# Split attention probabilities: transposed by TensorE, or laid out by one transposing DMA a head

## The chip, the cores and the metric

One core of a Trainium2 chip runs the kernel. The metric is the device time of one execution in microseconds (us); smaller is better. Engines are called as the profile calls them: PE is TensorE (PEld its weight loads), ACT ScalarE, DVE VectorE, POOL GpSimd, SP SyncE, whose queue (SPq) issues all DMAs here.

## The reference

Thirty-two batches of 256 tokens with 512 features, and 16 heads of 32 features each:

```python
h = jnp.maximum(_layernorm(x, axis=-1), 0.0)
q = split_heads(h @ Wq.T); k = split_heads(h @ Wk.T); v = split_heads(h @ Wv.T)
bias = (adj + adj)[:, None]
a = jnp.einsum('bhnd,bhmd->bhnm', q, k) * scale + bias
row_nonzero = jnp.any(a != 0, axis=-1, keepdims=True)
a = jnp.where(row_nonzero, a, -jnp.inf)
p = jax.nn.softmax(a, axis=-1)
p = jnp.where(jnp.isnan(p), 0.0, p)
o = jnp.einsum('bhnm,bhmd->bhnd', p, v)
x = x + (o @ Wo.T)
```

## The kernel before, in words

Precision comes from splitting: each operand of a product is kept as a high part and a low part, and three products are added (high by high, high by low, low by high). A split takes two passes: ACT copies the value rounded (`..._hi`), DVE subtracts that from the value (`..._lo`).

The work of a batch is laid out in 16 **slots**, one a head, and each engine has its own hand-written queue of slots (`body` in the block of each engine). In slot hh:

- PE transposes the probabilities of head hh into PSUM (`transpose_probs`, L401, four 128x128 blocks), computes the scores of head hh + 3 (`scores`, L390), in even slots the values of heads hh - 2 and hh - 1 (`values`, L422 and L423, 16 small f16 matmuls for two heads), and then the piece of the projections that the table `JOBS` gives this slot (`job`, L328). A job is a tuple (kind, number, batch offset, first product, end): `qk` is a projection to queries and keys of four heads (24 products of 256 columns), `v` a part of the values (12 products), `y` half of the output projection (12 products of 512 columns), `h` and `o` transposes of the normalised tokens and of the attention output.
- DVE adds the adjacency to the scores of head hh + 2 and finds the row bound (`shift`, L703), does its half of the splits of the jobs that ended in the slot before (`take`), and then the low half of the probabilities of head hh (`low_probs`, L721).
- ACT copies finished values out of PSUM in odd slots (`copy_outputs`, L542), takes the exponentials of head hh + 1 (`exponentials`, L553, two instructions, one for each 128 rows), does its half of the takes (L519, L520 for `qk`), and then the high half of the probabilities of head hh (`high_probs`, L564).
- POOL folds the shifted scores for the test of empty rows (`fold`), divides by the row sums (`divide`), normalises the next tokens and adds the residual.
- SP loads and stores, and rearranges finished queries and keys into `qk_stack` (`stack`, L252): twice a batch, 12 DMAs in one piece, each to 32 partitions.

The exponentials write an SBUF tile `probs` of two buffers. PE transposes from it into the PSUM tile `pT_ps` of two banks, and both halves of the split are made there and land in `pT_hi` and `pT_lo` (f16, four buffers each), the stationary operands of `values`. What orders the heads is this: the exponentials of head n + 1 wait for the transposes of head n - 1,

```python
act.wait_ge(pT_ready, head_no(b, hh) - 1)
```

and those of head n for the split of head n - 2. PSUM has eight banks: three for scores, two for `pT_ps`, one for the values, two for jobs.

## Time and profile before

| | |
|---|---|
| median of 3 runs | 1320.17 us (1317.58 to 1320.48) |
| the profiled execution's own time | 1319.87 us |
| its span | 1318.1 us |
| busy in the span | PE 1288.6 us (98%), DVE 1130.4 (86%), ACT 1033.8 (78%), POOL 902.1 (68%) |
| DMA engines | 47.9% of 16 engines' span, for 163.64 MB |
| granted clock of PE | 0.996 of full speed, mean over the run |

The profile gives one execution. Busy times are unions of the instructions' spans: two instructions of one engine can overlap by some 0.1 us, so the distance from one start to the next is what an instruction costs its engine, and its own span is when its result is there. The 32 batches make a steady loop; a short stretch in front splits the weights and fills the pipeline, and one behind drains it.

### The profile page before, as it was taken

How to read it: one execution, taken by the hardware profiler on the slowest of the kernel's cores; microseconds unless marked ns; L12 is line 12 of the kernel's file. 1: busy time of each engine (PE TensorE's matmuls, PEld its weight loads, DVE VectorE, ACT ScalarE, POOL GpSimd, SP SyncE). 2: the span in 40 equal slices, each digit the busy share in tenths (PEclk: the TensorE clock that was granted, in tenths of full speed). 3: DMA queues.
4: the chain of work that ended last, by engine and by line, in shares of the span. 5: the costliest groups of instructions: out<-in, count | busy, mean ns of one | idle time of the engine just before them, and what ended most of it. 6: DMA issues, size and time to landing. Idle time of an engine off the chain costs nothing. (4 is left out here: it accounts for less than half of the span.)

```text
span 1318.1 us, 43774 instructions
## 1 busy us (share of the span) xinstructions
PE 1288.6 (98%) x13072; PEld 1225.6 (93%) x13072; DVE 1130.4 (86%) x4023; ACT 1033.8 (78%) x2379; POOL 902.1 (68%) x1263
## 2 busy tenths in 40 slices
PE   5899999999999999999999999999999999999996
PEld 5899999999999999999999999999999999999995
DVE  5888888888888888888889888888888888888884
ACT  3788778788787888887888787888788887788874
POOL 5667667667677676676776676776677776676765
PEclk9999999999999999999999999999999999999998
DMA  6445454455354454454454454454544554544441
GB/s 213 104 117 138 108 136 119 115 139 127 109 146 117 109 148 119 112 143 116 114 151 109 122 130 121 123 143 108 131 119 122 133 133 110 139 119 113 126 121 49
DMA packets 90772, 163.88 MB, mean 124 GB/s; under 512 B 14976, under 2 KB 23168, under 8 KB 90752
## 3 DMA queue, kind: packets, MB, share of 16 engines
q1 hardware_dynamic: 90752, 163.64, 47.9%
q8 instruction: 10, 0.16, 0.1%
q14 instruction: 10, 0.08, 0.0%
HBM read 46.14 MB, written 16.78 MB: 48 GB/s over the span
## 5 line engine op out<-in xcount | busy, mean ns | idle before, releaser
L849 POOL TENSOR_TENSOR fold<-minus 128x512 f32<-128x512 f32 x256 | 329.7, 1288 | 325.3 <-DVE bounds L703 325.3
L553 ACT ACTIVATE probs<-minus,bounds 128x256 f32<-128x256 f32 x1024 | 460.2, 500 | 19.1 <-DVE bounds L703 19.1
L564 ACT ACTIVATE pT_hi<-pT_ps 128x512 f16<-128x512 f32 x512 | 306.0, 598 | 154.3 <-PE pT_ps L401 152.6
L721 DVE TENSOR_TENSOR pT_lo<-pT_ps,pT_hi 128x512 f16<-128x512 f32 x512 | 351.1, 686 | 84.5 <-ACT pT_hi L564 84.2
L703 DVE CUSTOM_DVE_ANT_0 minus<-s_ps,adj_now 128x256 f32<-128x256 f32 x1024 | 389.3, 417 | 18.3 <-DVE adj_now L715 14.3
L401 PE MATMUL pT_ps<-ident,probs 128*128 128x128 f32 x2048 | 307.6, 273 | 1.7 <-ACT probs L553 1.6
L328 PE MATMUL job_ps<-hT_hi,w_hi 128*128 128x256 f32 x1024 | 300.4, 293 | 3.1 <-DVE hT_lo L671 2.6
L328 PE MATMUL job_ps<-hT_lo,w_hi 128*128 128x256 f32 x1024 | 290.1, 283 | 0.0
L328 PE MATMUL job_ps<-hT_hi,w_lo 128*128 128x256 f32 x1024 | 289.8, 283 | 0.0
L401 PEld LDWEIGHTS pT_ps<-ident,probs 128*128 128x128 f32 x2048 | 240.4, 140 | 15.4 <-ACT probs L553 2.6
L390 PE MATMUL s_ps<-qk_stack 96*128 96x256 f32 x1024 | 247.1, 323 | 2.2 <-DMA qk_stack<-qk_parts 2.2
L855 POOL TENSOR_TENSOR bounds<-fold 128x256 f32<-128x256 f32 x256 | 189.3, 740 | 24.9 <-POOL fold L849 9.5
L328 PEld LDWEIGHTS job_ps<-hT_hi,w_hi 128*128 128x128 f32 x1024 | 194.8, 190 | 3.8 <-issue 3.8
L328 PEld LDWEIGHTS job_ps<-hT_hi,w_lo 128*128 128x128 f32 x1024 | 196.0, 191 | 0.0
L328 PEld LDWEIGHTS job_ps<-hT_lo,w_hi 128*128 128x128 f32 x1024 | 195.8, 191 | 0.0
L390 PEld LDWEIGHTS s_ps<-qk_stack 96*128 96x128 f32 x1024 | 154.8, 191 | 2.7 <-DMA qk_stack<-qk_parts 2.6
L422 PE MATMUL o_ps<-v_parts,pT_hi 128*128 128x65 f16 x2048 | 153.6, 192 | 1.4 <-DVE pT_lo L721 1.0
L423 PE MATMUL o_ps<-v_parts,pT_lo 128*128 128x33 f16 x2048 | 147.5, 179 | 0.0
L328 PE MATMUL job_ps<-w_hi,hT_lo 128*128 128x256 f32 x512 | 147.4, 288 | 0.0
L328 PE MATMUL job_ps<-w_hi,hT_hi 128*128 128x256 f32 x512 | 147.3, 288 | 0.1
L328 PE MATMUL job_ps<-w_lo,hT_hi 128*128 128x256 f32 x512 | 144.3, 282 | 0.0
L422 PEld LDWEIGHTS o_ps<-v_parts,pT_hi 128*128 128x128 f16 x2048 | 123.6, 96 | 14.3 <-DVE pT_lo L721 1.5
(80 smaller groups left out, 2406.4 us busy)
## 6 DMA issues: line engine op xcount, KB each, us to landing
qk_stack<-qk_parts SPq DMA_DIRECT2D x768, 128.0 KB, 2.3
x_in<-x SPq DMA_DIRECT2D x32, 512.0 KB, 3.4
x_res<-x SPq DMA_DIRECT2D x32, 512.0 KB, 3.6
out<-y SPq DMA_DIRECT2D x64, 256.0 KB, 2.1
adj_in<-adj SPq DMA_DIRECT2D x32, 256.0 KB, 3.6
minus<-wq_t SPq DMA_DIRECT2D x2, 512.0 KB, 6.0
qk_parts<-wv SPq DMA_DIRECT2D x2, 512.0 KB, 10.5
y<-wk_t SPq DMA_DIRECT2D x1, 512.0 KB, 8.4
```

The source lines that it names most:

```text
L328: end = nc.tensor.matmul(dst, lhs[a](k), rhs[c](k), start=i == 0, stop=i == len(terms) - 1)
L390: end = nc.tensor.matmul(s_ps[SCORE_BANK[hh]][:, t * N:(t + 1) * N], stack[:, 0, t * P:(t + 1) * P], stack[:, 1, :], start=True, stop=True)
L401: end = nc.tensor.transpose(pT_ps[hh % 2][:, m * N + t * P:m * N + (t + 1) * P], probs[hh % 2][:, t, m * P:(m + 1) * P], ident[:, :])
L422: nc.tensor.matmul(ps[:, 0:LOW + HD], hi, v[:, 0:LOW + HD], start=m == 0, stop=False)
L423: end = nc.tensor.matmul(ps[:, 0:HD + 1], lo, v[:, 0:HD + 1], start=False, stop=m == NT - 1)
L553: end = nc.scalar.activation(probs[hh % 2][:, t, :], minus[hh // 2 % 2][:, hh % 2, t, :], ACT.Exp, bias=bounds[:, hh // 2 % 4, 2 * (hh % 2 ...
L564: nc.scalar.activation(pT_hi[hh % 4][:, :, :], pT_ps[hh % 2][:, :].rearrange("p (m n) -> p m n", m=NT), ACT.Copy).then_inc(pT_high, 1)
L703: end = nc.vector.tensor_tensor_reduce(out=minus[pair % 2][:, hh % 2, t, :], in0=s_ps[SCORE_BANK[hh]][:, t * N:(t + 1) * N], in1=adj_now[: ...
L721: nc.vector.tensor_tensor(pT_lo[hh % 4][:, :, :], pT_ps[hh % 2][:, :].rearrange("p (m n) -> p m n", m=NT), pT_hi[hh % 4][:, :, :], ALU.sub ...
L849: nc.gpsimd.tensor_tensor(f1[:, :, :], src[:, :, 0:N // 2], src[:, :, N // 2:N], ALU.add).then_inc(folded1, 1)
L855: nc.gpsimd.tensor_tensor(f2, f1[:, :, 0:N // 4], f1[:, :, N // 4:N // 2], ALU.add).then_inc(folded2, 1)
```

## The change

- The exponentials write to PSUM (`probs`, two banks, in the natural layout: rows on partitions). ACT copies the high half from there and DVE subtracts the low half into one SBUF tile `p_parts` (f16, both halves, four buffers).
- SP then issues one transposing DMA a head (`turn_probs`): it reads `p_parts` (128 partitions, 1024 f16 each, 256 KB) and writes `pT` as eight blocks of 128x128, what `values` takes as stationary operands. PE's `transpose_probs` is gone. `values` runs two slots later (heads hh - 4 and hh - 3), and with it `copy_outputs`, `any_nonzero`, `factors` and `divide`.
- Scores have two banks in place of three, jobs three in place of two.
- The products of `qk` and `v` take f16 operands: `hT`, and the weights scaled to powers of two. For it, all three of Wq, Wk, Wv are scaled by rows and transposed by PE in the stretch in front, as only Wv was before.
- The table of jobs is new. `qk` jobs now end in slots 1, 7, 9 and 11, `v` jobs in 2, 3 and 15 (two), `o` in 6 and 14, `y` in 12 and 13. The copy of the adjacency moves from DVE to ACT, in slot 13; the statistics of the tokens on DVE move from slot 0 to slot 6.
- SP's queue carries the 16 transposing DMAs of a batch in slot order; the two bursts of stack DMAs stand behind those of heads 1 and 9.

```diff
-PRODUCTS = {"qk": 24, "v": 12, "y": 12, "h": 1, "o": 1}
+W_TOP, H_TOP = 2.0 ** 14, 2.0 ** 9
+PRODUCTS = {"qk": 24, "v": 12, "y": 12, "h": 4, "o": 4}
 JOBS = {
-    0: [("qk", 3, 0, 0, 12)],
-    1: [("qk", 3, 0, 12, 24), ("v", 2, 0, 0, 2)],
+    0: [("qk", 3, 0, 0, 13)],
+    1: [("qk", 3, 0, 13, 24), ("v", 2, 0, 0, 2)],
     2: [("v", 2, 0, 2, 12), ("v", 3, 0, 0, 3)],
...
+    6: [("qk", 0, 1, 6, 16), ("o", 1, -1, 0, 4)],
+    7: [("qk", 0, 1, 16, 24), ("qk", 1, 1, 0, 6)],
+    8: [("qk", 1, 1, 6, 18)],
...
+            def turn_probs(b, hh, early):
+                sp.wait_ge(p_split, head_no(b, hh) + 1)
+                settled(sp, "sp")
+                if not early:
+                    sp.wait_ge(pv_done, head_no(b, hh) - 3)
+                    settled(sp, "sp")
+                sp.dma_start_transpose(pT[hh % 4][:, :, :],
+                                       p_parts[hh % 4][:, :, :, :].rearrange("p a t n -> p (a t n)")
+                                       ).then_inc(p_turned[hh % 4], 16)
             def body(b, first, last):
-                if not last:
-                    sp.wait_ge(adj_copied, b + 1)
-                    settled(sp, "sp")
-                    sp.dma_start(adj_in[:, :, :], adj_d[b + 1]).then_inc(adj_loaded, 16)
-                stack(1, b, first)
-                if not (last or isinstance(b, int) and b + 2 == B):
-                    load_tokens(b + 2)
-                if not first:
-                    store(b - 1, 0)
-                if not last:
-                    stack(0, b + 1, False)
-                if not first:
-                    store(b - 1, 1)
-                    sp.dma_start(x_res[:, :, :], x_d[b]).then_inc(res_loaded, 16)
+                for hh in range(HEADS):
+                    turn_probs(b, hh, first and hh < 4)
+                    if hh == 0 and not last:
+                        sp.wait_ge(adj_copied, b + 1)
+                        settled(sp, "sp")
+                        sp.dma_start(adj_in[:, :, :], adj_d[b + 1]).then_inc(adj_loaded, 16)
+                        if not (isinstance(b, int) and b + 2 == B):
+                            load_tokens(b + 2)
+                    if hh == 1:
+                        stack(1, b, first)
+                    if hh == 9 and not last:
+                        stack(0, b + 1, False)
+                    if hh == 14 and not first:
+                        store(b - 1, 0)
+                    if hh == 15 and not first:
+                        store(b - 1, 1)
+                        sp.dma_start(x_res[:, :, :], x_d[b]).then_inc(res_loaded, 16)
...
-            def transpose_probs(b, hh, early):
-                pe.wait_ge(exp_done, head_no(b, hh) + 1)
-                if not early:
-                    pe.wait_ge(pT_split, head_no(b, hh) - 1)
-                for m in range(NT):
-                    for t in range(NT):
-                        end = nc.tensor.transpose(pT_ps[hh % 2][:, m * N + t * P:m * N + (t + 1) * P],
-                                                  probs[hh % 2][:, t, m * P:(m + 1) * P], ident[:, :])
-                end.then_inc(pT_ready, 1)
...
-                pe.wait_ge(pT_split, head_no(b, hh) + 1)
+                pe.wait_ge(p_turned[hh % 4], b * HEADS * 4 + (hh // 4 + 1) * 16)
                 for t in range(NT):
                     q = (hh % 2) * NT + t
                     ps = o_ps[:, q * P:(q + 1) * P]
                     for m in range(NT):
-                        hi = pT_hi[hh % 4][:, m, t * P:(t + 1) * P]
-                        lo = pT_lo[hh % 4][:, m, t * P:(t + 1) * P]
+                        hi, lo = (pT[hh % 4][:, (part * NT + t) * NT + m, :] for part in range(2))
...
-                    for was in range(hh - 2, hh) if hh % 2 == 0 else ():
...
+            def scale_weight(i, half):
+                act.wait_ge(w_scales, TURNS.index((i, half)) + 1)
+                for k in range(2 * half, 2 * half + 2):
+                    end = nc.scalar.activation(w_in[i][:, k, :], w_in[i][:, k, :], ACT.Copy,
+                                               scale=w_scale[:, i, UNSCALE, k:k + 1])
+                end.then_inc(w_scaled, 1)
...
                 if not early:
-                    act.wait_ge(pT_ready, head_no(b, hh) - 1)
+                    act.wait_ge(p_split, head_no(b, hh) - 1)
                 for t in range(NT):
-                    end = nc.scalar.activation(probs[hh % 2][:, t, :], minus[hh // 2 % 2][:, hh % 2, t, :], ACT.Exp,
+                    end = nc.scalar.activation(probs[hh % 2][:, t * N:(t + 1) * N], minus[hh // 2 % 2][:, hh % 2, t, :], ACT.Exp,
                                                bias=bounds[:, hh // 2 % 4, 2 * (hh % 2) + t, BOUND:BOUND + 1],
                                                scale=-1.0)
                 end.then_inc(exp_done, 1)
             def high_probs(b, hh, early):
-                act.wait_ge(pT_ready, head_no(b, hh) + 1)
+                act.wait_ge(exp_done, head_no(b, hh) + 1)
                 if not early:
-                    act.wait_ge(pv_done, head_no(b, hh) - 3)
-                nc.scalar.activation(pT_hi[hh % 4][:, :, :], pT_ps[hh % 2][:, :].rearrange("p (m n) -> p m n", m=NT),
-                                     ACT.Copy).then_inc(pT_high, 1)
-            for half in range(2):
-                high_weight(WQ, half)
-            high_weight(WK, 0)
+                    act.wait_ge(p_turned[hh % 4], b * HEADS * 4 + hh // 4 * 16)
+                nc.scalar.activation(p_parts[hh % 4][:, 0, :, :], probs[hh % 2][:, :].rearrange("p (t n) -> p t n", t=NT),
+                                     ACT.Copy).then_inc(p_high, 1)
...
+                act.wait_ge(adj_loaded, (b + 1) * 16)
+                if not (isinstance(b, int) and b == 0):
+                    act.wait_ge(shifted, head_no(b, 0))
+                nc.scalar.activation(adj_now[:, :, :], adj_in[:, :, :], ACT.Copy).then_inc(adj_copied, 1)
...
+                    if hh == HEADS - 3 and not last:
+                        copy_adj(b + 1)
                     high_probs(b, hh, first and hh < 4)
+                    for kind, n, d in ended_in(hh, first, last):
+                        take(kind, n, b + d)
...
-            def low_probs(b, hh, early):
-                dve.wait_ge(pT_high, head_no(b, hh) + 1)
-                nc.vector.tensor_tensor(pT_lo[hh % 4][:, :, :], pT_ps[hh % 2][:, :].rearrange("p (m n) -> p m n", m=NT),
-                                        pT_hi[hh % 4][:, :, :], ALU.subtract).then_inc(pT_split, 1)
+            def low_probs(b, hh):
+                dve.wait_ge(p_high, head_no(b, hh) + 1)
+                nc.vector.tensor_tensor(p_parts[hh % 4][:, 1, :, :], probs[hh % 2][:, :].rearrange("p (t n) -> p t n", t=NT),
+                                        p_parts[hh % 4][:, 0, :, :], ALU.subtract).then_inc(p_split, 1)
```

The first place is ACT's queue in a slot in which a `qk` job is taken. Numbers behind tile names are buffers, and what a row waits for stands in brackets. Before:

```order
L553 ACTIVATE probs1<-minus1,bounds 128x256 [waits pT_ready,shifted]
L553 ACTIVATE probs1<-minus1,bounds 128x256
L514 REGISTER_ALU
L519 ACTIVATE qk_parts<-job_ps0 128x256 [waits ended_qk]
L520 ACTIVATE qk_parts<-job_ps0 128x256
L563 REGISTER_ALU [waits pT_ready]
L564 ACTIVATE pT_hi2<-pT_ps0 128x512 [waits pv_done]
```

And in the changed kernel:

```order
L570 ACTIVATE probs1<-minus1,bounds 128x256 [waits p_split,shifted]
L570 ACTIVATE probs1<-minus1,bounds 128x256
L530 REGISTER_ALU
L535 ACTIVATE qk_parts<-job_ps2,q_scale 128x256 [waits ended_qk]
L537 ACTIVATE qk_parts<-job_ps2 128x256
L581 ACTIVATE p_parts2<-probs0 128x512 [waits p_turned2,exp_done]
```

The order of the three pieces stayed; the exponentials now wait for `p_split`, which DVE raises at the end of its low half, where they waited for PE's transposes, and the high half waits for the transposing DMA that last read its buffer.

The second place is SP's queue at the head of a batch. Before:

```order
L280 DMA adj_in<-adj 128x2x256
L244 ISA
L248 REGISTER_ALU [waits taken_qk]
L252 DMA qk_stack<-qk_parts 32x1024 [waits scores_ready]
L252 DMA qk_stack<-qk_parts 32x2x512 x2
```

And in the changed kernel:

```order
L283 DMA_TRANSPOSE pT1<-p_parts1 128x8x128 [waits pv_done]
L242 ISA
L250 DMA qk_stack<-qk_parts 32x1024 [waits taken_qk,scores_ready]
L250 DMA qk_stack<-qk_parts 32x2x512 x2
L250 DMA qk_stack<-qk_parts 32x1024
L250 DMA qk_stack<-qk_parts 32x2x512 x2
L250 DMA qk_stack<-qk_parts 32x1024
L250 DMA qk_stack<-qk_parts 32x2x512 x2
L250 DMA qk_stack<-qk_parts 32x1024
L250 DMA qk_stack<-qk_parts 32x2x512 x2
L277 REGISTER_ALU
L281 REGISTER_ALU [waits p_split]
L283 DMA_TRANSPOSE pT2<-p_parts2 128x8x128 [waits pv_done]
```

The transposing DMA of head 2 now stands behind the 12 stack DMAs and behind their wait for the takes of `qk`.

## Rows read from the trace of the kernel before

**Rows 1.** Busy time by engine in one batch's stretch; columns as named:

```profile
core 0: us, PE busy (x) PEld busy (x) DVE busy (x) ACT busy (x) POOL busy (x), PEclk, DMA share, GB/s
600.00:640.00 40.00, 40.00 (x412) 38.20 (x411) 35.08 (x128) 32.04 (x74) 27.80 (x41) 1.00 0.49 125
```

**Rows 2.** Timeline of PE: start us, duration us, engine, line, operation:

```profile
619.73 0.60 PE L401 MATMUL pT_ps<-ident,probs 128*128 128x128 f32 x4
620.09 0.48 PE L390 MATMUL s_ps<-qk_stack 96*128 96x256 f32 x2
620.41 0.28 PE L328 MATMUL job_ps<-hT_hi,w_hi 128*128 128x256 f32 x1
620.53 0.28 PE L328 MATMUL job_ps<-hT_lo,w_hi 128*128 128x256 f32 x1
...
622.51 0.20 PE L422 MATMUL o_ps<-v_parts,pT_hi 128*128 128x65 f16 x1
...
622.97 0.48 PE L328 MATMUL job_ps<-w_hi,oT_hi 128*128 128x512 f32 x1
```

**Rows 3.** Timeline of ACT and DVE through one slot with a `qk` take:

```profile
650.70 0.60 ACT L564 ACTIVATE pT_hi<-pT_ps 128x512 f16<-128x512 f32 x1 [0.70 <-PE pT_ps L401]
651.19 0.90 ACT L553 ACTIVATE probs<-minus,bounds 128x256 f32<-128x256 f32 x2
651.33 0.69 DVE L721 TENSOR_TENSOR pT_lo<-pT_ps,pT_hi 128x512 f16<-128x512 f32 x1 [0.54 <-ACT pT_hi L564]
...
652.36 0.38 ACT L519 ACTIVATE qk_parts<-job_ps 128x256 fp32r<-128x256 f32 x1 [0.27 <-PE job_ps L328]
...
652.64 0.38 ACT L520 ACTIVATE qk_parts<-job_ps 128x256 fp32r<-128x256 f32 x1
...
652.90 0.60 ACT L564 ACTIVATE pT_hi<-pT_ps 128x512 f16<-128x512 f32 x1
653.05 0.42 DVE L677 SCALAR_TENSOR_TENSOR qk_parts<-job_ps,qk_parts 128x256 fp32r<-128x256 f32 x1 [0.35 <-ACT qk_parts L520]
653.39 0.41 DVE L679 TENSOR_TENSOR qk_parts<-job_ps,qk_parts 128x256 fp32r<-128x256 f32 x1
...
653.72 0.68 DVE L721 TENSOR_TENSOR pT_lo<-pT_ps,pT_hi 128x512 f16<-128x512 f32 x1
```

**Rows 4.** Groups of instructions of DVE, 600 to 1000 us (ten batches):

```profile
L688 DVE TENSOR_TENSOR oT_lo<-job_ps,oT_hi 128x512 fp32r<-128x512 f32 x20 | 13.6, 682 | 0.0
...
L614 DVE BATCH_NORM_STATS2 stats<-x_in 128x6 f32<-128x512 f32 x20 | 12.8, 679 | 0.0
...
L715 DVE COPY adj_now<-adj_in 128x512 f32<-128x512 f32 x10 | 9.1, 910 | 0.0
```

**Rows 5.** Timeline of SP's queue over one batch: the issues:

```profile
631.13 0.40 SPq L280 DMA_DIRECT2D adj_in<-adj  x1
...
658.79 7.70 SPq L252 DMA_DIRECT2D qk_stack<-qk_parts  x12
...
669.86 0.41 SPq L291 DMA_DIRECT2D x_res<-x  x1
670.96 0.40 SPq L280 DMA_DIRECT2D adj_in<-adj  x1
```

**Rows 6.** The page's DMA issues: count, KB each, median us to landing:

```profile
qk_stack<-qk_parts SPq DMA_DIRECT2D x768, 128.0 KB, 2.3
...
out<-y SPq DMA_DIRECT2D x64, 256.0 KB, 2.1
adj_in<-adj SPq DMA_DIRECT2D x32, 256.0 KB, 3.6
```

**Rows 7.** Six us inside a burst of stack DMAs, columns as in Rows 1:

```profile
680.00:686.00 6.00, 6.00 (x56) 5.41 (x56) 5.47 (x23) 5.08 (x12) 5.46 (x8) 1.00 0.84 192
```

**Rows 8.** SP's queue in front, with the weight loads still under way:

```profile
6.01 3.02 SPq L268 DMA_DIRECT2D adj_in<-adj  x1
```

**Rows 9.** Busy time and granted clock in two stretches in front, as Rows 1:

```profile
35.00:37.00 2.00, 1.12 (x8) 0.88 (x9) 1.79 (x6) 2.00 (x6) 1.73 (x2) 0.98 0.84 213
37.00:39.00 2.00, 2.00 (x12) 2.00 (x10) 1.55 (x5) 0.18 (x1) 0.00 (x0) 0.50 0.02 8
```

More of the change, by code:

```diff
@@ L71, in ended_before, with ended_in, attention_block @@
     if hh:
-        return [j[:3] for j in jobs_at(hh - 1, first, last) if j[4] == PRODUCTS[j[0]]]
+        return [j[:3] for j in jobs_at(hh - 1, first, last)
+                if j[4] == PRODUCTS[j[0]] and j[:2] not in TAKEN_AT_ONCE]
     return [(kind, n, d - 1) for kind, n, d, _, end in JOBS[HEADS - 1]
-            if end == PRODUCTS[kind] and not (first and d < 1)]
-def attention_block(nc, x, adj, wq_t, wk_t, wv, wo_t, out):
+            if end == PRODUCTS[kind] and not (first and (d < 1 or (kind, n) == ("v", 0)))]
+def ended_in(hh, first, last):
+    return [j[:3] for j in jobs_at(hh, first, last) if j[:2] in TAKEN_AT_ONCE]
+def attention_block(nc, x, adj, wq, wk, wv, wo_t, out):
     B, N, D = x.shape
@@ L143, in attention_block @@
         o_raw = [sb(f"o_raw{i}", [P, 2 * NT, VW - 1]) for i in range(2)]
[L144 to L146 removed]
+        p_parts = [sb(f"p_parts{i}", [P, 2, NT, N], F16) for i in range(4)]
+        pT = [sb(f"pT{i}", [P, 2 * NT * NT, P], F16) for i in range(4)]
         o = sb("o", [P, NT, D])
@@ L463, in body @@
                         scores(b + 1, hh + AHEAD - HEADS)
-                    for was in range(hh - 2, hh) if hh % 2 == 0 else ():
+                    for was in range(hh - 4, hh - 2) if hh % 2 == 0 else ():
                         if was >= 0:
@@ L602, in _ @@
             body(B - 1, False, True)
-            copy_outputs(B - 1, PAIRS - 1, False)
+            for pair in range(PAIRS - 2, PAIRS):
+                copy_outputs(B - 1, pair, False)
             take("o", 1, B - 1)
@@ new lines, in low_weight @@
+            def low_weight(i, half):
+                at = TURNS.index((i, half))
+                dve.wait_ge(w_high, at + 1)
+                for j in range(2):
+                    cols = slice(half * HALF, (half + 1) * HALF)
+                    end = nc.vector.tensor_tensor(
+                        w_lo[i][:, 2 * j:2 * j + 2, cols],
+                        turn_ps[at % 2][j][:, :].rearrange("p (k n) -> p k n", k=2),
+                        w_hi[i][:, 2 * j:2 * j + 2, cols], ALU.subtract)
@@ L778, in body @@
                     if pair:
-                        factors(*pair, first and hh < 6)
-                    low_probs(b, hh, first and hh < 2)
-                    if not last and hh == 0:
-                        moments_of(b + 1)
-            body(0, True, False)
-            with dve.Fori(1, B - 1) as b:
-                body(b, False, False)
-            body(B - 1, False, True)
-            any_nonzero(B - 1, PAIRS - 1)
-            factors(B - 1, PAIRS - 1, False)
+                        factors(*pair, first and hh < 9)
+                    low_probs(b, hh)
+                    for kind, n, d in ended_in(hh, first, last):
+                        take(kind, n, b + d)
+                    if not (last or nearly) and hh == 6:
+                        moments_of(b + 2)
+            body(0, True, False, False)
+            with dve.Fori(1, B - 2) as b:
+                body(b, False, False, False)
+            body(B - 2, False, True, False)
+            body(B - 1, False, False, True)
+            for pair in range(PAIRS - 2, PAIRS):
+                any_nonzero(B - 1, pair)
+                factors(B - 1, pair, False)
             take("o", 1, B - 1)
```

395 lines of the change are left out of this document (203 added, 192 removed), and 23 rows, old and new, of the table JOBS.

## The prediction

> **What bounds the kernel now.** I read the busy times of one batch's stretch first, then PE's timeline, then ACT and DVE side by side through one slot, last SP's queue. In 40 us PE is busy for all 40, DVE for 35.1, ACT for 32.0, POOL for 27.8, at full clock [rows 1]; PE's timeline has no hole, and each instruction starts where the one before lets it [rows 2]. So PE is the bound and a batch lasts as long as its instructions: from one `adj_in` issue to the next, 631.13 to 670.96, 39.83 us [rows 5]. 32 of these are 1274.6 us; the span is 1318.1, so the stretch in front and the tail cost 43.5 together. The profiled execution took 1319.87 us, 1.8 more than its span and 0.3 less than the median of the runs, 1320.17. The sum below is made against 1319.87.
>
> **PE's part.** Four transposes of probabilities hold PE from 619.73 to 620.09 us, 0.36 us a head [rows 2]; 16 heads give 5.8 us a batch, and they go. A product of 256 columns costs 0.12 us from start to start [rows 2]. What f16 makes of it no row shows, since only the small products of `values` are f16: 16 of them, eight of 65 and eight of 33 columns, take 0.46 us [rows 2], 0.33 of it columns at 2.4 GHz (784 columns), so 8 ns each on top; 256 columns are 0.107 us, and 0.115 with those 8 ns. Between 0.107 and 0.12 I take 0.115: 144 products of `qk` and `v` a batch save 0.7 us (0 to 1.9). PE's own work falls to 39.8 - 5.8 - 0.7 = 33.3 us. The adjacency copy, 0.91 us [rows 4], leaves DVE, which is then busy for 35.1 - 0.9 = 34.2. If engines only had to be busy, a batch would take a little over 34 us. I don't believe it, for what the order of the queues does.
>
> **The ring between ACT and DVE.** Before, the exponentials waited for PE's transposes, done well ahead. Now `probs` itself is the PSUM tile that both halves are split from, with two banks, so the exponentials of head n + 1 wait for `p_split` of head n - 1, and ACT's queue puts the high half of head n behind them. That closes a ring, one turn a head: high half (ACT), low half (DVE), exponentials (ACT), high half. Its pieces: the high half ends 0.60 us after its start, and DVE's low half starts 0.03 us after that end (650.70 + 0.60, then 651.33); the low half lasts 0.69; ACT starts after some 0.03 again; the pair of exponentials holds ACT for two starts of about 0.40, 0.80 in all (a pair is 0.90 long, and its last 0.10 overlaps what follows, as 0.60 is 0.49 from start to start, 650.70 to 651.19) [rows 3]. One turn is 0.60 + 0.03 + 0.69 + 0.03 + 0.80 = 2.15 us, 34.4 us a batch, with nothing else in it. But the takes stand between the exponentials and the high half:
> - `qk`, four a batch. ACT's two copies are 0.28 us each from start to start; DVE begins its two subtractions when the second has ended and holds them for 0.67 us, ahead of the low half (652.64, 653.05, 653.72) [rows 3]. From the start of the exponentials: 0.80 + 0.28 + 0.38 + 0.03 = 1.49, and the low half at 2.16 where it would start at 1.43. 4 x 0.73 = 2.9 us.
> - `v`, four, one ACT copy of 0.28: 1.1 us. `y`, two, one of 0.49: 1.0. The adjacency copy, now ACT's, 128x512 as the high half is: 0.5.
> - `o`, two. DVE's subtraction lasts 0.68 [rows 4] and holds DVE 0.60; it can start at 0.80 + 0.60 + 0.03 = 1.43, the low half at 2.03: 2 x 0.60 = 1.2.
> - the token statistics, two of 0.68 [rows 4] and two small ones, stand behind the low half of head 6, ahead of head 7's: I count 1.1 us of these 1.6 as late.
> `copy_outputs` and the `h` takes fall into the wait for the low half and cost nothing; without that cover they would cost 3 and 1 us. Sum: 34.4 + 2.9 + 1.1 + 1.0 + 0.5 + 1.2 + 1.1 = 42.2 us a batch, above the 39.8 of now, with PE idle in a fifth of it. The unknown in it is the write of the exponentials to PSUM instead of SBUF, which no row shows; the nearest rows (650.70 against 651.19) are an instruction that reads PSUM, and they allow 0.40 a start to be 0.35 to 0.45, -1.6 to +1.6 us a batch. By the Trainium skill (ScalarE: Activation LUTs, What happens when an `exp` ACTIVATE runs) ScalarE writes faster to PSUM than to SBUF; no row here shows that, and it would move this term towards its lower end.
>
> **The transposing DMA.** SP's queue now holds in a batch 24 stack DMAs (12 issue in 7.70 us, so 15.4) and five others of some 0.4, 17.4 us [rows 5], and 16 transposing ones. What one costs to issue, no row shows: at least the 0.40 of a plain DMA of 256 KB [rows 5], at most the 3.02 of one that found the engines full [rows 8]. A DMA to 32 partitions costs 0.64 [rows 5]; eight blocks of 128x128 look more like that and more. Moving 256 KB at the rate of a burst, 192 GB/s at 84% busy [rows 7], is 262/229 = 1.15 us of all engines. I take 1.1 us for the issue. Landing: 2.1 to 3.6 us after the issue for plain 256 KB [rows 6]; I take 3.
>
> In plain slots this is hidden: the values need head n three slots later. Not at the two bursts. Let head 1's split be at 0. SP issues its transpose until 1.1, waits for the `qk` takes until about 2.3, issues 12 stack DMAs until 10.0, and only then head 2's transpose, which lands, behind the stack's own transfers, at about 13.4. Head 6 needs that buffer for its high half, which the ring would reach after the turns of heads 2 to 5 (2.9 + 2.4 + 2.4 + 2.2 = 9.9) and the exponentials (0.8 and a hand-over), so at about 11. The ring stands still for 2.4 us, PE's values of head 2 for longer. Heads 9 and 10 repeat it: 4.8 us a batch. A batch then takes 42.2 + 4.8 = 47.0 us. DMA engines: 0.479 x 39.8 = 19 us plus 16 x 1.15 = 18, together 37 of 47, not the bound.
>
> **In front and behind.** Wq and Wk join Wv in being scaled, transposed and split in two passes before the first scores, and two pairs more hang behind the last transpose. I add 10 and 3 us, an estimate (0 to 20). Sum: 32 x 47.0 + 43.5 + 13 = 1560.5, and 1.8 outside the span: **1562 us**, 18% over now.
>
> **Rivals.**
> - *SP's issue is the bound.* If one transposing DMA costs T to issue, a batch can't be shorter than 17.4 + 16 T; this passes 47.0 at T = 1.85. At 2.1 it gives 51.0 us a batch, 1690 us; at 3.02, 65.7 and 2160. For it: SP is one queue, and the shape is new; against it: 256 KB now issue in 0.40. The Trainium skill (DMA: Bandwidth & Descriptors, the table of DmaTranspose costs) gives 262,144 sequencer cycles for 8,192 tiles in the older generations, one push a tile, or 32 cycles each; with tiles of 16 rows by 128 elements and 1.2 GHz, 64 tiles would be an estimate of 1.7 us an issue; each burst would stand some 1 us longer, and the sum by it would be some 1620 us. The page on VectorE (VectorE: DVE Perf Modes, The three transpose paths) names TensorE as the path to choose where PSUM will do.
> - *The ring alone.* The transposes land early enough that the bursts stop nothing: 42.2 x 32 + 56.5 + 1.8 = 1409 us.
> - *PE's clock falls.* It was at 0.50 for two us after a stretch in which PE was busy for 1.1 of 2 us [rows 9]. The stops at the bursts are longer than that. A few us at half clock after each cost 1 to 2 us a batch, some 40 us; were it at 1.2 GHz throughout, 33.3 us would be some 62, and the time about 2050.
> - *Faster.* One mechanism, the ring turns quicker than I say: it must lose 2.4 of 42.2 us, 0.15 us a head, by a PSUM write that takes 0.33 and not 0.40, and the bursts must stop nothing. Then the next bound is DVE, 34.2 us; if a turn lost 0.3 us, 37.4 us a batch, 1255 us. For it: 5.8 us of PE's work do go. Against it: 0.60 and 0.69 are measured for these very shapes from PSUM.
> - *It doesn't do what it says*: no room for this, the transposes are gone from PE's queue and the waits stand in the order of the queues.
>
> **How the numbers follow.** Ring and bursts, as summed, 1450 to 1620: 0.60. Ring alone: 0.13. SP's issue as the bound: 0.13, of which about half below 1690. Clock low throughout: 0.03. Faster: 0.08. No change to within 0.2%, about what a measurement of this kernel can tell: 0.03, a ring that turns in just 39.8 us. The range from 1400 to 1690 us leaves out faster, no change, the low clock and the slower half of the issue case, about 0.2. Slower by over 0.2%: 0.89.
>
> **What would show it.** In the profile after: ACT's `probs` waits for DVE's `p_parts` (not for its bounds) in nearly every slot, 0.7 us and more each; PE has idle time, and its `o_ps` waits for DMA `pT` twice a batch by some us; a batch lasts 47 us from one `adj_in` issue to the next; SP shows 1.1 us for a DMA_TRANSPOSE. Wrong would be: PE gapless as now, or ACT's waits small; SP solid with transposes would speak for the issue rival, a batch of 42 without waits for `pT` for the ring alone.

## The result, and the profile after

| | before | after |
|---|---|---|
| median of the runs, us | 1318.88 | 1691.61 |
| lowest to highest | 1317.37 to 1320.48 | 1689.01 to 1692.97 |
| span of the profiled execution, us | 1318.1 | 1690.3 |
| one batch, `adj_in` issue to `adj_in` issue, us | 39.8 [rows 5] | 51.20 |
| mean granted clock of PE in the profiled execution | 0.996 | 0.855 |

After over before is 1.2824, 95% interval 1.2798 to 1.2849: 28% slower, where 18% was predicted, and 1.6 us above the upper end of the range. A batch is the mean of twelve here (507.64 to 1122.06), and of all complete periods between 500 and 1150 us for the kernels below. A slot is measured from one start of ACT's exponentials to the next.

From the page of the changed kernel, busy time and count by engine, two rows of the 40 slices, and the groups that hold the story (busy us, mean ns, idle before, releaser):

```profile
PE 1241.9 (73%) x11056; PEld 989.6 (59%) x11056; DVE 1140.7 (67%) x4006; ACT 1039.1 (61%) x2427; POOL 883.1 (52%) x1262
...
PE   5676876877876877877777767778768768778766
...
PEclk8888988888879888889889889789888888898886
...
L570 ACT ACTIVATE probs<-minus,bounds 128x256 f32<-128x256 f32 x1024 | 447.1, 469 | 339.3 <-DVE p_parts L754 337.3
L754 DVE TENSOR_TENSOR p_parts<-probs,p_parts 128x512 f16<-128x512 f32 x512 | 351.7, 687 | 196.0 <-ACT p_parts L581 181.1
L427 PE MATMUL o_ps<-v_parts,pT 128*128 128x65 f16 x2048 | 177.4, 199 | 345.1 <-DMA pT<-p_parts 308.0
...
L581 ACT ACTIVATE p_parts<-probs 128x512 f16<-128x512 f32 x512 | 300.3, 587 | 85.4 <-DMA pT<-p_parts 85.4
...
pT<-p_parts SPq DMA_TRANSPOSE x512, 2.8
```

No engine is near full, and PE no longer is either [rows 1]. The exponentials wait for the low half (337 us), the low half for the high half (181), the values for the transposing DMA (308). ACT's high half waits 85 us for a DMA too, to get its buffer back. SP's queue over one batch (start, length):

```profile
712.76 0.40 SPq L294 DMA_DIRECT2D adj_in<-adj  x1
713.50 0.37 SPq L258 DMA_DIRECT2D x_in<-x  x1
714.18 1.24 SPq L283 DMA_TRANSPOSE pT<-p_parts  x1
715.79 7.80 SPq L250 DMA_DIRECT2D qk_stack<-qk_parts  x12
723.92 16.54 SPq L283 DMA_TRANSPOSE pT<-p_parts  x8
741.79 7.67 SPq L250 DMA_DIRECT2D qk_stack<-qk_parts  x12
749.73 7.38 SPq L283 DMA_TRANSPOSE pT<-p_parts  x5
...
```

A transposing DMA costs SP 1.24 us, and where the splits are long done a start comes every 1.50 (behind the burst at 723.92, 725.47, 726.95, 728.43 and 729.92): the other quarter lies between two issues. The first of these lands at 726.71, 2.8 us after its issue. What PE did behind the first burst, in windows of 2 us (columns as in rows 1):

```profile
722.00:724.00 2.00, 1.02 (x8) 0.71 (x7) 1.80 (x9) 1.20 (x4) 1.38 (x2) 1.00 0.95 215
724.00:726.00 2.00, 0.00 (x0) 0.00 (x0) 1.14 (x5) 0.82 (x2) 1.38 (x3) 0.86 0.89 202
726.00:728.00 2.00, 0.49 (x8) 0.39 (x8) 0.58 (x1) 0.60 (x1) 0.00 (x0) 0.50 0.67 149
728.00:730.00 2.00, 1.76 (x15) 1.37 (x16) 1.81 (x6) 1.15 (x3) 0.00 (x0) 0.50 0.78 178
730.00:732.00 2.00, 2.00 (x12) 1.74 (x10) 0.96 (x6) 0.22 (x1) 1.32 (x2) 0.50 0.91 206
732.00:734.00 2.00, 2.00 (x17) 1.56 (x16) 1.59 (x4) 1.00 (x3) 1.36 (x3) 0.93 0.05 9
```

PE stands from 723.0 to 726.84, and then runs at 0.50, 1.2 GHz, for some six us. ACT's timeline in the same stretch (the bracket is the idle time and its releaser) shows how one late DMA is paid more than once:

```profile
726.79 0.60 ACT L581 ACTIVATE p_parts<-probs 128x512 f16<-128x512 f32 x1 [1.97 <-DMA pT<-p_parts]
728.79 0.39 ACT L559 ACTIVATE o_raw<-o_ps 128x260 f32<-128x260 f32 x1 [1.41 <-PE o_ps L428]
729.08 0.87 ACT L570 ACTIVATE probs<-minus,bounds 128x256 f32<-128x256 f32 x2
731.78 0.60 ACT L548 ACTIVATE oT_hi<-job_ps 128x512 fp32r<-128x512 f32 x1 [1.84 <-PE job_ps L383]
```

The high half of head 6 waits 1.97 us for the buffer that the DMA of head 2 still reads. Then the copy of the output sums, in front of the exponentials in ACT's queue, waits 1.41 us for values whose own DMA (head 3's) has just landed, and the copy of an `o` job waits 1.84 us for transposes that PE, late and at half clock, has not done. At the second burst of the same batch the wait for the buffer is short, and PE's lateness is the larger part:

```profile
752.58 0.60 ACT L581 ACTIVATE p_parts<-probs 128x512 f16<-128x512 f32 x1 [0.45 <-DMA pT<-p_parts]
...
754.65 0.39 ACT L559 ACTIVATE o_raw<-o_ps 128x260 f32<-128x260 f32 x1 [1.48 <-PE o_ps L428]
...
760.42 0.39 ACT L544 ACTIVATE v_parts<-job_ps 128x256 f16<-128x256 f32 x1 [1.45 <-PE job_ps L343]
```

### The profile page after: what moved, and what is told of

The parts are those of the page before. It is cut to its first block and busy times, and to the rows that moved or that the text cites. A ratio compares the mean times of both kernels' runs of the same rounds, so it can differ in the third digit from the quotient of the medians.

```text
span 1690.3 us, 41253 instructions
## 1 busy us (share of the span) xinstructions
PE 1241.9 (73%) x11056; PEld 989.6 (59%) x11056; DVE 1140.7 (67%) x4006; ACT 1039.1 (61%) x2427; POOL 883.1 (52%) x1262
## 5 line engine op out<-in xcount | busy, mean ns | idle before, releaser
L754 DVE TENSOR_TENSOR p_parts<-probs,p_parts 128x512 f16<-128x512 f32 x512 | 351.7, 687 | 196.0 <-ACT p_parts L581 181.1
L427 PE MATMUL o_ps<-v_parts,pT 128*128 128x65 f16 x2048 | 177.4, 199 | 345.1 <-DMA pT<-p_parts 308.0
L427 PEld LDWEIGHTS o_ps<-v_parts,pT 128*128 128x128 f16 x2048 | 137.1, 103 | 391.5 <-issue 291.5
L581 ACT ACTIVATE p_parts<-probs 128x512 f16<-128x512 f32 x512 | 300.3, 587 | 85.4 <-DMA pT<-p_parts 85.4
L343 PE MATMUL job_ps<-hT_hi,w_hi 128*128 128x256 f16 x1024 | 298.9, 292 | 9.3 <-DVE hT_lo L709 6.8
L343 PE MATMUL job_ps<-hT_lo,w_hi 128*128 128x256 f16 x1024 | 299.1, 292 | 0.0
L343 PE MATMUL job_ps<-hT_hi,w_lo 128*128 128x256 f16 x1024 | 296.6, 290 | 0.0
L428 PE MATMUL o_ps<-v_parts,pT 128*128 128x33 f16 x2048 | 171.0, 187 | 0.0
L343 PE MATMUL job_ps<-w_hi,hT_hi 128*128 128x256 f16 x512 | 170.1, 332 | 0.0
L343 PE MATMUL job_ps<-w_lo,hT_hi 128*128 128x256 f16 x512 | 168.3, 329 | 0.0
L428 PEld LDWEIGHTS o_ps<-v_parts,pT 128*128 128x128 f16 x2048 | 140.1, 99 | 0.0
```

The source lines that it names most:

```text
L343: end = nc.tensor.matmul(dst, lhs[a](k), rhs[c](k), start=i == 0, stop=i == len(terms) - 1)
L427: nc.tensor.matmul(ps[:, 0:LOW + HD], hi, v[:, 0:LOW + HD], start=m == 0, stop=False)
L428: end = nc.tensor.matmul(ps[:, 0:HD + 1], lo, v[:, 0:HD + 1], start=False, stop=m == NT - 1)
L581: nc.scalar.activation(p_parts[hh % 4][:, 0, :, :], probs[hh % 2][:, :].rearrange("p (t n) -> p t n", t=NT), ACT.Copy).then_inc(p_high, 1)
L754: nc.vector.tensor_tensor(p_parts[hh % 4][:, 1, :, :], probs[hh % 2][:, :].rearrange("p (t n) -> p t n", t=NT), p_parts[hh % 4][:, 0, :, : ...
```

## The experiments

Twelve kernels ran. The edits are against the changed kernel unless said otherwise, and only their main lines are shown. Three kernels (`e6_ring`, `e11_free`, `e12_free_bulk`) leave out the stack DMAs of all batches but the first, so their later batches work on the queries and keys of the first: their times tell what waits for what, and they are not kernels to use.

**The queue and the ring, one at a time.** `e1_spread` spreads the stack DMAs:

```diff
...
-                    if hh == 1:
-                        stack(1, b, first)
-                    if hh == 9 and not last:
-                        stack(0, b + 1, False)
+                    if 1 <= hh <= 4:
+                        stack(1, b, first, [hh - 1])
+                    if 9 <= hh <= 12 and not last:
+                        stack(0, b + 1, False, [hh - 9])
```

> Each burst of 12 stack DMAs is cut into four groups of three, one behind the transposing DMAs of heads 1 to 4 and of 9 to 12; all else as in the changed kernel (1692 us, 51.0 us a batch). If bursts in SP's queue are a large part of the loss (PE and ACT wait for a late transpose twice a batch, and PE's clock falls behind each stop), the stops of 4 us go and a batch takes 46 to 48 us, 1530 to 1600 us in all. If the ring between ACT and DVE is all of it, nothing changes, 1690. If SP's issue in sum is the bound, nothing changes either, since SP issues the same.

Measured: 1561.52 us, ratio 1.1825 [1.1805, 1.1844], a batch 47.00 us, clock 0.916. That is 130 us for the placing of 24 DMAs a batch, none of them taken away, and within what was expected. It isn't the whole price of the bursts, for one new stop a batch came with it, in slot 4 (PE, then ACT):

```profile
762.92 0.24 PE L427 MATMUL o_ps<-v_parts,pT 128*128 128x65 f16 x1 [3.47 <-DMA pT<-p_parts]
764.40 0.60 ACT L532 ACTIVATE hT_hi<-job_ps 128x512 f16<-128x512 f32 x1 [3.02 <-PE job_ps L358]
```

The values wait for head 1's DMA, issued at 757.50 behind the two bulk loads. Slot 4 lasts 5.0 us in the mean, where it has 2.5 in the changed kernel and 2.7 in `e6_ring` below; the other slots are within 0.1 us of those of `e6_ring`. `e2_four` cuts the ring and leaves the bursts:

```diff
-                    act.wait_ge(p_split, head_no(b, hh) - 1)
+                    act.wait_ge(p_split, head_no(b, hh) - 3)
...
-                    end = nc.scalar.activation(probs[hh % 2][:, t * N:(t + 1) * N], minus[hh // 2 % 2][:, hh % 2, t, :], ACT.Exp,
+                    end = nc.scalar.activation(p_sb[hh % 4][:, t, :], minus[hh // 2 % 2][:, hh % 2, t, :], ACT.Exp,
...
```

> Ring opened, bursts kept: the exponentials write one of four SBUF tiles in place of one of two PSUM banks and wait for the split of head n - 4 in place of n - 2. If the ring is the larger part, it falls to 1450 to 1550 us and ACT's waits for DVE's p_parts vanish. If the bursts hold the time, heads behind a late transpose wait all the same and it stays within 1600 to 1690. A split read from SBUF may also cost ACT and DVE a little more or less by itself.

Measured: 1611.07 us, ratio 1.2194 [1.2159, 1.2230], a batch 48.55. ACT's exponentials no longer wait for the low half; what waits are the values and the high halves, both for the DMA (waits of PE and ACT over 600 to 1000 us: total, times, longest):

```profile
PE o_ps L428 <- DMA pT<-p_parts: 89.4, 41, 4.4
...
ACT p_parts L582 <- DMA pT<-p_parts: 45.8, 16, 3.8
```

In the changed kernel these two were 74.7 and 20.9 us. So part of the wait moved from the ring to the DMA, and the time lies where it was expected if the bursts hold it. `e3_both` has both edits.

> Both at once: four SBUF tiles and the stack DMAs spread. Ring and bursts as the two causes: 42 to 44 us a batch, 1390 to 1450 us, held now by SP's own queue, which issues 16 transposes at 1.49 us from start to start and 17.4 us of other DMAs, 41.2 us a batch, 1375 us at the least. If neither is a cause, 1690. Should it come below 1319, the transposing DMA would be worth its price; I don't expect it.

Measured: 1518.66 us, ratio 1.1494 [1.1457, 1.1530], a batch 45.73: 173 us less than the changed kernel, still 200 above before and 69 above the upper end of what was expected. Something else bounded, which `e7_bulk`, `e11_free` and `e12_free_bulk` name.

**The place of the exponentials** differs in `e2_four` as well as the wait. `e4_sbuf2` changes the place alone:

```diff
+        p_sb = [sb(f"p_sb{i}", [P, NT, N]) for i in range(2)]
...
-                    end = nc.scalar.activation(probs[hh % 2][:, t * N:(t + 1) * N], minus[hh // 2 % 2][:, hh % 2, t, :], ACT.Exp,
+                    end = nc.scalar.activation(p_sb[hh % 2][:, t, :], minus[hh // 2 % 2][:, hh % 2, t, :], ACT.Exp,
...
```

> The changed kernel with the exponentials in two SBUF tiles in place of the two PSUM banks, and the same waits (the exponentials of a head wait for the split of the head two before). It tells what the place alone does in e2_four, where four tiles gave -80 us though VectorE's subtraction took 928 ns from SBUF against 687 from PSUM. Theory A (the wait for the split is what cost the 80 us, and the place is only a price): 1690 to 1760 us, up to 16 x 32 x 0.24 = 123 us above the changed kernel if each slower subtraction lay in the ring. Theory B (the place was the gain): 1610 to 1650.

Measured: 1706.09 us, ratio 1.2933 [1.2911, 1.2954], 14 us above the changed kernel: theory A. So the place was no gain, and the 80 us of `e2_four` are the wait's, net of that price. (The 928 ns are the subtraction in `e3_both`; in `e2_four` it has 871 in the mean.)

**The ring alone.** `e6_ring`:

```diff
             def stack(half, b, first):
+                if not (isinstance(b, int) and b == 0):
+                    return
...
-                if hh % HH < G:
+                if hh % HH < G and isinstance(b, int) and b == 0:
```

> All the transposing DMAs stay, and the stack transfers (24 a batch, 15.5 us of SP) are issued for the first batch alone, which leaves that part of the work out: the later batches take the stacks of the first. What is left is the ring of ScalarE, VectorE and TensorE without a burst on SP's queue. Theory A (the prediction's ring of 42.2 us a batch was right, and all above it comes from the queue): 32 x 42.2 + 43.5 + 13 = about 1409 us, taken as 1390 to 1440, at a granted clock of 0.97 or more. Theory B (the ring itself was undersized, since exponentials that wait for the split and a 2.8 us landing cost more a slot): 1480 us or more.

Measured: 1487.49 us, ratio 1.1272 [1.1253, 1.1291], clock 0.954, a batch 44.69. Above both 1409 and the band around it: theory B, by 2.5 us a batch. ACT and DVE through a slot with a `qk` take, in time order:

```profile
653.77 0.87 ACT L572 ACTIVATE probs<-minus,bounds 128x256 f32<-128x256 f32 x2 [0.82 <-DVE p_parts L756]
...
654.59 0.45 ACT L537 ACTIVATE qk_parts<-job_ps,q_scale 128x256 fp32r<-128x256 f32 x1
654.95 0.37 ACT L539 ACTIVATE qk_parts<-job_ps 128x256 fp32r<-128x256 f32 x1
655.21 0.59 ACT L583 ACTIVATE p_parts<-probs 128x512 f16<-128x512 f32 x1
655.35 0.48 DVE L717 SCALAR_TENSOR_TENSOR qk_parts<-job_ps,q_scale,qk_parts 128x256 fp32r<-128x256 f32 x1 [0.98 <-ACT qk_parts L539]
...
655.75 0.41 DVE L719 SCALAR_TENSOR_TENSOR qk_parts<-job_ps,qk_parts 128x256 fp32r<-128x256 f32 x1
656.08 0.68 DVE L756 TENSOR_TENSOR p_parts<-probs,p_parts 128x512 f16<-128x512 f32 x1
```

The next exponentials start at 656.85, so this slot lasts 3.08 us, and 0.93 of it is above the summed turn of 2.15, where I had 0.73: the query's copy with its scale now takes 0.36 us from start to start and its subtraction 0.40, against 0.28 and 0.34 before [rows 3]. Read the same way, a plain turn is 2.20, one with a `v` take 2.48, with an `o` take 2.87. Slot 5 is longer for a thing that I had at nothing: DVE comes to the low half of head 5 late (641.42), since it is busy, but for 0.20 us, with the low half of head 4, an `h` take, the scores' minimum and the three small operations of a pair (from 638.74 on); that slot is 2.68 (2.72 in the mean). The slot with the statistics and an `o` take is 4.09, 0.24 above its sum, and slot 4 is 2.70 in the mean, 0.22 above a plain turn with a `v` take: there PE waits some 1.2 us a batch for head 1's DMA.

**PE's clock.** `e5_warm` puts 30 products of no use (128x256, f16) ahead of PE's wait behind each burst, so that PE stands less.

```diff
+                    if hh in (6, 14):
+                        keep_warm(hh, b, first, last)
...
+                for _ in range(30):
+                    nc.tensor.matmul(job_ps[i][:, 0:N], hT_hi[:, 0, 0:P], hT_hi[:, 1, :], start=True, stop=True)
```

> 30 products of 256 columns that nobody reads are put ahead of PE's waits for head 2 and head 10 (3.3 us of work each at full clock, into the bank of the next o job), where PE stands idle for about 4 us now. They leave nothing out and add PE work. If PE's fall to 0.5 of its clock behind each stop costs 2 us a batch or more, the time falls by 40 to 100 us and the clock's mean rises from 0.855 to above 0.93. If the clock costs nothing, since PE waits anyway, the time stays or rises by up to 30 us.

Measured: 1630.35 us, ratio 1.2354 [1.2334, 1.2375], clock 0.948. PE is busy for 110 us more and the kernel 61 us faster. PE's timeline, the filler and what follows it:

```profile
918.78 3.45 PE L439 MATMUL job_ps<-hT_hi 128*128 128x256 f16 x30 [0.24 <-ACT y L563]
922.43 0.19 PE L427 MATMUL o_ps<-v_parts,pT 128*128 128x65 f16 x1 [0.20 <-DMA pT<-p_parts]
923.82 0.20 PE L427 MATMUL o_ps<-v_parts,pT 128*128 128x65 f16 x1 [1.02 <-DMA pT<-p_parts]
```

The wait for the DMA is as long as ever, only filled. So the half clock was at least 61 us of the changed kernel, 1.9 a batch (the clock's mean is still 0.948, not 0.996); in the sum of bursts below it is contained.

**By the DMA or by the block.** `e8_halves` cuts each transposing DMA into two of four blocks.

```diff
-                sp.dma_start_transpose(pT[hh % 4][:, :, :],
...
+                for part in range(2):
+                    sp.dma_start_transpose(pT[hh % 4][:, 4 * part:4 * part + 4, :],
...
```

> The changed kernel with each transposing DMA of eight 128x128 blocks cut into two of four blocks, high half and low half. It tells whether an issue costs by the DMA or by the block. By the block: each issue lasts some 0.65 us, and with about 0.25 us between instructions a batch of SP's queue grows by 16 x 0.25 = 4 us, to some 1700 to 1820 us. By the DMA: each lasts 1.25 as now, SP needs 17.4 + 32 x 1.49 = 65 us a batch, some 2140 us.

Measured: 2111.62 us (one execution), a batch 64.44 (65 by the second account, 2140 us). SP's queue, two halves together:

```profile
1018.97 1.25 SPq L284 DMA_TRANSPOSE pT<-p_parts  x1
1020.50 7.72 SPq L250 DMA_DIRECT2D qk_stack<-qk_parts  x12
1028.55 2.55 SPq L284 DMA_TRANSPOSE pT<-p_parts  x2
```

Half the blocks cost SP the same time. At these sizes the issue is paid by the DMA. The Trainium skill (DMA: Bandwidth & Descriptors, the table of DmaTranspose costs), which I had used for an estimate, has one push a tile in the older generations; four blocks should then have taken half of eight, and they don't.

**The bulk loads in front of the first burst.** `e7_bulk` is `e3_both` with the loads elsewhere:

```diff
-                    if hh == 0 and not last:
+                    if hh == 6 and not last:
...
                         sp.dma_start(adj_in[:, :, :], adj_d[b + 1]).then_inc(adj_loaded, 16)
-                        if not (isinstance(b, int) and b + 2 == B):
-                            load_tokens(b + 2)
...
+                    if hh == 13 and not (isinstance(b, int) and b + 3 >= B):
+                        load_tokens(b + 3)
```

> e3_both (groups of three stack transfers, four tiles for the exponentials; 1518.7 us) with the two bulk loads moved: adj_in from behind the transposing DMA of head 0 to behind that of head 6, x_in to behind that of head 13 of the batch before, so that neither stands before the groups of stack transfers. Theory A (the transposing DMA of head 1 lands 5.2 us after its issue there, behind these loads, and that stalls all engines once a batch): the stall of some 2 us and the half clock behind it go, 50 to 100 us in all, to 1420 to 1470. Theory B (SP's time is what counts, wherever the loads stand): within 15 us of 1519.

Measured: 1509.34 us, ratio 1.1439 [1.1417, 1.1460], a batch 45.39. Only 9 us: theory B. The waits of SP's queue over 400 us say why:

```profile
SPq L214 <- DVE qk_parts L721: 0.4, 1, 0.4
SPq L214 <- DVE p_parts L758: 0.3, 1, 0.3
```

SP hardly waits, 0.7 us in 400 (55.4 in the changed kernel): here the first rival of the prediction, SP's issue as the bound, is real. Of the 400 us its issues hold 328, 37.3 a batch; the other 8 a batch are SP's own steps between them, of which the 41.2 in the expectation of `e3_both` counts about half. The DMA engines are busy for 0.88 of the time there, but the issues are not held up by them: a transposing one has 1.29 us in the mean, for 1.24 in the changed kernel. To see whether that holds, `e11_free` and `e12_free_bulk` take the stack DMAs out of `e3_both` and of `e7_bulk`, by the edit of `e6_ring`.

> e3_both (four SBUF tiles for the exponentials, so no ring) with the stack transfers issued for the first batch alone, which leaves that work out: the transposing DMAs stay, SP's queue has room. Theory A (with the ring cut, SP's queue is the bound: in e7_bulk it never waits and a batch lasts 45.3 us): without 15.5 us of issue a batch SP needs some 28 us, and the bound goes to VectorE, 34 to 38 us busy with its slower subtraction from SBUF, so 37 to 41 us a batch, 1240 to 1370 us. Theory B (the landing of the transposes or VectorE's slower subtraction bounds, not the queue): above 1440 us.

> e11_free (no ring, stack transfers for the first batch alone) with adj_in loaded behind the transposing DMA of head 6 and x_in behind that of head 13 of the batch before, as in e7_bulk. In e11_free a batch lasts 42.36 us, and once in it the transposing DMA of head 1, issued 0.7 us behind these two loads, lands 5.3 us after its issue; TensorE stands 2.4 us for it and then runs at a granted clock of 0.50 for some 6 us. Theory A (a transposing DMA behind bulk loads lands late, and that stop is paid in full, as SP's queue no longer hides it): 1.5 to 4 us a batch less, 1280 to 1360 us. Theory B (the stop is hidden, or it follows the loads wherever they stand): within 20 us of 1406.

Measured: `e11_free` 1406.16 us, ratio 1.0665 [1.0646, 1.0684], a batch 42.28, between the two bands; `e12_free_bulk` 1339.01 us, ratio 1.0153 [1.0136, 1.0170], a batch 40.02, as theory A had it. So `e3_both` lost 112 us to the stack DMAs, `e7_bulk` 170, and `e11_free` another 67 to one transposing DMA a batch that lands 5.3 us after its issue, behind two loads. (Without the stack DMAs their landings and their share of the DMA engines are gone too, not their issue alone.) That one stop in `e11_free`, in windows of 2 us (columns as in rows 1; DMA share and GB/s last):

```profile
642.00:644.00 2.00, 1.57 (x15) 0.85 (x12) 2.00 (x10) 1.68 (x5) 1.22 (x1) 1.00 0.89 239
644.00:646.00 2.00, 0.03 (x2) 0.00 (x0) 2.00 (x7) 0.43 (x1) 1.76 (x4) 0.85 1.24 286
646.00:648.00 2.00, 1.59 (x13) 1.58 (x14) 0.23 (x1) 0.10 (x1) 0.49 (x1) 0.50 0.93 205
```

In `e12_free_bulk` PE's waits for `pT` are 0.4 us in 400, and DVE is the busiest engine with 93% of the span. Even without ring, bursts and late landings, and with the stack's work left out, the way by the DMA does not reach the time of before in this arrangement. What holds it there is in part the four SBUF tiles: DVE's low half takes 977 ns from them where it has 687 from PSUM, 4.6 us a batch (see the last section). No run had a source in PSUM and no ring, and none issued a part of the DMAs from another engine.

**The other half of the change.** `e9_pe` undoes the probability part and keeps the f16 products and the table.

```diff
...
-                    turn_probs(b, hh, first and hh < 4)
...
+                    transpose_probs(b, hh, first and hh < 2)
...
-                pe.wait_ge(p_turned[hh % 4], b * HEADS * 4 + (hh // 4 + 1) * 16)
+                pe.wait_ge(p_split, head_no(b, hh) + 1)
...
```

It is not the kernel before with one half of the change: the pairs of parts have eight buffers there, where before had four, and `values` keeps its place two slots later.

> The probability part is undone (TensorE transposes the exponentials into the two PSUM banks, with the exponentials in two SBUF tiles and eight pairs of parts; no transposing DMA), while the f16 products of the new table stay and the rest as well. Theory A (the DMA way of the transposes carries the whole loss, the f16 products carry none): about the time of the kernel before or below it, 1270 to 1325 us; with 144 products a batch at 0.109 in place of 0.12 us the gain is 32 x 144 x 0.011 = 50 us if TensorE bounds throughout. Theory B (the f16 products or the new table cost something of their own, by waits for the splits of the other heads): above 1340 us.

Measured: 1325.81 us, ratio 1.0050 [1.0034, 1.0067], a batch 39.85: 0.5% above before, and 0.8 us above the upper end of A. So the probability part alone is 366 of the changed kernel's 1692 us. PE's two waits there, over 400 us (ten batches):

```profile
PE job_ps L330 <- DVE oT_lo L726: 14.4, 10, 1.4
PE job_ps L330 <- DVE hT_lo L708: 2.6, 10, 0.3
```

PE works 38.3 us of 40 (before, all 40 [rows 1]): the f16 products do save 1.7 us a batch (1.6 by their price from start to start, below), and one wait of 1.44 with one of 0.26 takes it back. DVE's timeline shows what stands in front of the take it waits for:

```profile
614.24 1.27 DVE L652 BATCH_NORM_STATS2 stats<-x_in 128x6 f32<-128x512 f32 x2
...
617.07 0.67 DVE L726 TENSOR_TENSOR oT_lo<-job_ps,oT_hi 128x512 fp32r<-128x512 f32 x1
```

`e10_stats` is `e9_pe` with the statistics two slots later:

```diff
-                    if not (last or nearly) and hh == 6:
+                    if not (last or nearly) and hh == 8:
                         moments_of(b + 2)
...
-                    if not (last or nearly) and hh == 7:
+                    if not (last or nearly) and hh == 9:
                         normalise(b + 2, False)
```

> e9_pe with one thing more: VectorE's token statistics (1.6 us of VectorE) stand behind the low half of head 8 in place of head 6, and GpSimd's normalisation behind head 9 in place of 7. In e9_pe TensorE waits twice a batch and only twice, 1.44 us at the product of head 7's slot for VectorE's oT_lo, which comes late behind these statistics, and 0.26 us for hT_lo; a batch there lasts 39.84 us. Theory A (TensorE bounds again, the f16 products save what they save, and only this wait took it back): 1.4 to 1.7 us a batch less, 45 to 55 us in all, 1271 to 1283 us, below the kernel before. Theory B (VectorE or the two banks for scores are next in line, and the wait only moves): 1310 us or more.

Measured: 1280.60 us, ratio 0.9706 [0.9692, 0.9719], a batch 38.26: theory A, and 3% below before. PE's only wait that is left is the one for `hT_lo`, 0.26 a batch, and the page's row reads

```profile
PE 1233.4 (97%) x13104; PEld 1111.0 (87%) x13104; DVE 1111.7 (87%) x4006; ACT 1048.0 (82%) x2427; POOL 881.5 (69%) x1262
```

## Why the prediction was right and wrong

The sum had 32 x 47.0 + 56.5 + 1.8 = 1562. The profiled execution has 32 x 51.20 = 1638.4, 51.9 in front and behind (1690.3 less that), and 1.8 outside: 1692.1. The direction, the ring and the two stops a batch were right. Two terms of the sum were too small: the ring, by what stands in its turns, and the bursts, of which the prediction priced only one of two ways in which they stop the ring.

- **PE's part: right.** The transposes went, PE has holes. A product has 0.109 us from start to start (722.04, 722.14, 722.25), within the bounds 0.107 to 0.12; 144 of them save 1.6 us a batch at that price, where I took 0.7, and `e9_pe` shows 1.7.
- **The ring: right mechanism, 2.5 us a batch too small** (42.2; 44.7 in `e6_ring`), 80 us in all. What failed here is the size of its terms. Slot by slot, in the means of twelve batches of `e6_ring`: the plain turn, 2.15, came out at 2.20, and 0.05 a head is already 0.8 a batch. The write of the exponentials to PSUM, the unknown, was as good as taken (469 ns an instruction, 501 into SBUF in `e2_four`). A slot with a `qk` take is 0.93 above 2.15, for 0.73, which makes 0.6 a batch beyond the plain turn's share: I took the durations of before, and the diff adds a scale to the copy and to the subtraction of the query. The `h` takes I had at nothing behind the wait for the low half; slot 5 costs 0.5. That cover is ACT's: on DVE the take stands in front of the next slot's work, and there DVE had no idle time left. The statistics add 0.2 and head 1's late DMA, in slot 4, another 0.2.
- **The bursts: right mechanism, 1.7 us a batch too small** (4.8; 51.2 - 44.7 = 6.5), 54 us. When head 2's DMA would land I had at 13.4 us behind the split of head 1; DVE ended that split at 713.14 and the DMA landed at 726.71, 13.6. The issue of 1.1 us (1.24) was no great error. The step that failed here is "The ring stands still for 2.4 us, PE's values of head 2 for longer", with "Heads 9 and 10 repeat it". I priced the ring's wait for its buffer, twice 2.4, and left PE's lateness without a price. The wait for the buffer is 1.97 us at the first burst and 0.45 at the second, half of my 4.8: there the ring comes to the buffer only 13.1 us behind the split of head 9 (739.06), with the adjacency copy and two `y` takes in its way, for 11.7 at the first. The rest, over 4 us a batch, is PE's lateness, at a clock of 0.50 in part, since ACT's queue has the copies of PE's results in front of the exponentials: in the mean slot 6 is 2.9 us longer than in `e6_ring`, slot 7 by 0.7, and at the second burst slots 14 and 0 by 1.6 each, 6.8 together. That 4.8 stands as near to 6.5 as it does is thus in part luck: one piece too large hid a missing one. `e1_spread` agrees: with the bursts spread these four slots are back at the lengths of `e6_ring`.
- **PE's clock** stood among the rivals with "1 to 2 us a batch", and happened inside my likeliest case: at least 1.9 us by `e5_warm`. As a rival it could not move the sum. A stop that a case predicts, of a length at which the clock had fallen before [rows 9], has to carry the price in that same case.
- **SP's issue: wrong rival for this kernel, right one behind it.** At 1.49 us from start to start a batch needs 17.4 + 16 x 1.49 = 41.2 us of SP, 10 less than it lasts. By its formula it would need T = 2.1 for 51.2. But `e3_both`, `e7_bulk` and `e11_free` show that SP becomes the bound, at some 45 us, as soon as ring and bursts are gone. The estimate by the Trainium skill (DMA: Bandwidth & Descriptors, the table of DmaTranspose costs), 1.7 us, does not agree with the trace's 1.24; that its 1620 us are nearer to the time is luck.
- **In front and behind: right,** 52 and, in `e6_ring`, 57 for 56.5.
- **The range** took each undersized term as right: the case of ring and bursts, with a chance of 0.60, ended at 1620, 72 us below the time. It reached to 1690 for the issue rival's sake, and that this end was missed by only 1.6 is luck. The two terms make 134 us (80 and 54), of which the front gave 5 back: 129 of the 130 that were missing.

## What to carry to other kernels

Work that is taken from the bounding engine only helps if what replaces it, a DMA with its issue, its landing and its place in a queue full of bursts, is late for nobody; list for each late arrival every engine that has an in-order wait for it, and price each, with the clock that PE loses meanwhile. A change with two parts is best run as two: here one half cost 28%, and the other was worth 3% once a wait that it exposed was moved. After a faster step, look first at the one wait that took the gain back, and whether the instruction in front of it can stand elsewhere.

## What the runs showed of the hardware

- The issue of a transposing DMA holds SP for 1.2 us in the median, with eight blocks of 128x128 (`after`) and with four (`e8_halves`) alike. It lands 2.8 us after the issue (2.4 with four), and later behind 768 KB of plain loads: 4.5 us after its issue at 714.18 in `after`, 5.3 at the stop of `e11_free` shown above.
- DVE's low half takes 687 ns from PSUM, and 871 to 977 in the mean from SBUF, but not evenly. Two of them in `e11_free`, beside POOL, in time order:

```profile
663.41 0.68 DVE L758 TENSOR_TENSOR p_parts<-p_sb,p_parts 128x512 f16<-128x512 f32 x1
663.45 1.80 POOL L899 TENSOR_TENSOR fold<-minus 128x512 f32<-128x512 f32 x1
665.33 0.74 POOL L905 TENSOR_TENSOR bounds<-fold 128x256 f32<-128x256 f32 x1
665.39 1.22 DVE L758 TENSOR_TENSOR p_parts<-p_sb,p_parts 128x512 f16<-128x512 f32 x1
```

The one that starts first takes its usual time (0.68; 0.74), the other ends later by what it had to wait: POOL's fold takes 1.80 us, 1.27 in the mean of the changed kernel, and DVE's subtraction 1.22, of which 0.54 lie behind POOL's end at 666.07. The Trainium skill (SBUF — State Buffer, SBUF: two separate sides) says this of a VectorE operation with two SBUF inputs beside a GpSimd operation that reads SBUF: an exclusive lock for the whole instruction, where the loser waits. With the source in PSUM, as in the changed kernel, nothing of the kind shows: all 512 low halves take 677 to 693 ns. It is why four SBUF tiles were no clean test of the ring, and why `e4_sbuf2` was run.
